# Seven instead of five edge groups gathered from x itself, and SyncE's wait for stored tables moved to slot 5

## Time and profile before

| | |
|---|---|
| median of 3 runs | 1107.77 us (1105.65 to 1108.65) |
| profiled execution | 1106.27 us |
| its span | 1104.5 us |
| POOL, gathers (L1068) | 741 from 3.7 us on, the last at 945.8 us |
| TensorE busy | 989.4 us, 90% of the span |
| VectorE, ScalarE, POOL busy | 824.7, 667.3, 739.1 us |

### The profile page before, as it was taken

How to read it: one execution, slowest core, us unless ns; L and a number is a source line. 1 busy time by engine, 2 the same in 40 slices (tenths; PEclk the granted TensorE clock), 3 DMA queues, 4 the chain that set the end, 5 groups by cost and what they waited for, 6 DMA issues and landing times.

```text
span 1104.5 us, 25223 instructions
## 1 busy us (share of the span) xinstructions
PE 989.4 (90%) x7011; PEld 737.0 (67%) x7041; DVE 824.7 (75%) x2919; ACT 667.3 (60%) x1736; POOL 739.1 (67%) x794
## 2 busy tenths in 40 slices
PE   5768988989799999989999999997888889899997
PEld 4456766767577677766767766666656667656786
DVE  6577877878778877877878878886877878645465
ACT  3334777888878787878877877643333233312664
POOL 7667777777777777777777777777777777200332
PEclk9798899999989999999999999998999999999998
DMA  8553443344434443344353444433454454545221
GB/s 207 153 140 94 98 105 90 93 108 106 107 86 112 105 113 96 97 102 127 91 122 91 107 121 112 107 97 91 99 147 95 110 143 105 139 132 161 83 58 41
DMA packets 126663, 121.24 MB, mean 110 GB/s; under 512 B 24238, under 2 KB 111077, under 8 KB 126517
## 3 DMA queue, kind: packets, MB, share of 16 engines
q1 hardware_dynamic: 99704, 69.74, 23.6%
q0 software_dynamic: 23712, 48.61, 18.2%
q10 hardware_dynamic: 3101, 1.21, 0.4%
HBM read 105.60 MB, written 13.88 MB: 108 GB/s over the span
## 4 chain that ended last, share of the span: by engine, by line
POOL 42%; PE 31%; issue 16%; DMA 5%; DVE 3%; ACT 1%; SPq 1%; ACTq 1%; DVEq 0%
POOL area L1068 42%; PE bank L1913 7%; PE bank L1693 5%; PE bank L1760 4%; PE bank L1788 3%; PE bank L1682 3%; PE bank L1633 3%; PE bank L1672 2%; DMA area<-zs_d,area 2%; PE bank L1621 1%; DMA area<-zr_d 1%; DMA adj_w<-in_dst_dram 1%; SPq L478 1%; DVE area L1364 0%; DMA area<-parts_d 0%
## 5 line engine op out<-in xcount | busy, mean ns | idle before, releaser
L1068 POOL DMA_INDIRECT area<-zs_d,area x721 | 687.0, 953 | 226.8 <-issue 218.3
L1254 DVE TENSOR_TENSOR_SCAN area<-area,bank 128x512 f32<-128x512 bf16 x196 | 249.6, 1274 | 172.3 <-PE bank L1633 151.4
L870 ACT CAST adj_w<-bank 128x325 f32 x391 | 176.7, 452 | 321.2 <-PE bank L1693 256.3
L1238 DVE TENSOR_SCALAR area<-area 128x325 bf16<-128x325 f16 x782 | 251.4, 322 | 0.0
L1693 PE MATMUL bank<-area 128*128 128x104 f32 x1564 | 228.1, 289 | 0.2
L1237 DVE TENSOR_SCALAR area<-area 128x128 bf16<-128x128 f16 x782 | 208.6, 267 | 12.5 <-PE bank L1693 11.2
L1693 PEld LDWEIGHTS bank<-area 128*128 128x128 f32 x1564 | 199.1, 199 | 10.4 <-issue 1.5
L1633 PE MATMUL bank<-ident,area 128*128 128x128 f32 x726 | 123.3, 294 | 52.6 <-DMA area<-zs_d,area 52.3
L1682 PE MATMUL bank<-area 128*128 128x325 bf16 x782 | 153.6, 310 | 11.4 <-ACT area L871 6.5
L923 ACT ACTIVATE area<-adj_w,node_c 128x512 bf16<-128x512 f32 x225 | 155.1, 744 | 0.0
L1633 PEld LDWEIGHTS bank<-ident,area 128*128 128x128 f32 x726 | 78.6, 144 | 97.4 <-DMA area<-zs_d,area 67.3
(11 more groups left out here) (174 smaller groups left out, 1029.8 us busy)
## 6 DMA issues: line engine op xcount, KB each, us to landing
area<-mask_d SPq DMA_DIRECT2D x195, 128.0 KB
area<-zs_d,area POOLq DMA_INDIRECT x721
area<-zs_d SPq DMA_DIRECT2D x640, 0.5 KB
area<-parts_d SPq DMA_DIRECT2D x20, 384.0 KB, 7.8
area<-wp_d SPq DMA_DIRECT2D x195, 9.0 KB
zr_d<-area SPq DMA_DIRECT2D x24, 128.0 KB
area<-zr_d SPq DMA_DIRECT2D x6, 512.0 KB, 4.7
area<-scale_d SPq DMA_DIRECT2D x10, 256.0 KB, 4.8
```

The source lines that it names most:

```text
L870: nc.scalar.copy(adj[:, :, bass.ds(at, W)], A_BANK[s % 2][:, 0:COLS].rearrange("p (h w) -> p h w", w=W))
L1068: pool.indirect_dma_start(gring[:, g % GR * 4 + s % 2 * 2 + u, :], None, x if g < RAW else zs_d[0:N, :], bass.IndirectOffsetOnAxis(ap=firs ...
L1238: nc.vector.tensor_scalar(hot_d[:, r, u, :], i_key[:, 0:COLS], key_n[:, u, s:s + 1], None, ALU.is_equal)
L1254: nc.vector.tensor_tensor_scan(S[:, g % 2, 0:n], mask[:, g % MR, 0:n], (G_BANK if g in PICKED else T_BANK[g % 2])[:, 0:n], S[:, (g + 1) % ...
```

## The change

`RAW` is 7. Groups 5 and 6 are gathered from x ahead of POOL's wait for `zs_st` and its branch; their raw buffers are two unused stretches of `aggT`. `raw_T` and `copy_raw` of group 4 move from slot 3 to slot 2, where those of group 5 join them, and those of group 6 stand in slot 3; on both engines they are now the first work of the slot (on TensorE, `raw_T(4)` stood behind the half pieces before, of which there are none so early). POOL's rule for the ring follows `RAW`: groups 9 and 10 wait for `raw_ps`, `t_ps` counts from group 11 on. SyncE's waits for `wp_st` and `zs_st` move from ahead of its loop into slot 5, behind `load_edges(5)`.

```diff
-RAW = 5
+RAW = 7
+RAW_SLOTS = ((4, 2), (5, 2), (6, 3))
...
         def raw(g):
-            return aggT[:, 512 * g:512 * g + 512] if g < 3 else raw_l[:, g - 3, :]
+            a = 512 * (g if g < 3 else g - 2)
+            return raw_l[:, g - 3, :] if g in (3, 4) else aggT[:, a:a + 512]
@@ SyncE @@
-                sp.wait_ge(wp_st, 48 * (BB - 1))
-                sp.wait_ge(zs_st, 16 * NX)
                 for k in range(NG + 5):
                     if 2 <= k < NG:
                         load_edges(k)
+                    if k == 5:
+                        sp.wait_ge(wp_st, 48 * (BB - 1))
+                        sp.wait_ge(zs_st, 16 * NX)
@@ ScalarE @@
                 for k in range(SLOTS):
-                    if k == 3:
-                        copy_raw(4)
+                    for g, at in RAW_SLOTS:
+                        if at == k:
+                            copy_raw(g)
                     if slots(k, 2) is not None:
                         adjacent(k - 2)
@@ TensorE @@
                 for k in range(SLOTS):
+                    for g, at in RAW_SLOTS:
+                        if at == k:
+                            raw_T(g)
...
-                    if k == 3:
-                        raw_T(4)
                     if 2 <= k < NG:
                         rows_T(k)
```

## The result

The changed kernel took 1109.1 us (median of 22 runs, 1107.18 to 1112.88) against 1107.64 us (22 runs) for the kernel before. The ratio is 1.0018, 95% interval 1.0009 to 1.0026: 1.0 to 2.9 us slower, inside the 0.3% that was called no change and inside the forecast range.

The account below looks back on a forecast made before the run. POOL's gathers bound the kernel; of 7.0 us of gaps 5.0 can go, but late rows_T waits leave D - 0.82 = +0.6 us: 1106.27 to 1106.9, or 1108.4 against the median. Range 1105.0 to 1111.0, 8 in 10.

Parts of the forecast that it names:

- No change that can be told, slightly slower, and why: Whole kernel: POOL's gain at groups 5 to 13 is lost waiting at 11 and 14; +0.6 us, chance 0.72.
- the part on what is late next: POOL at groups 11, 14, 15: waits for rows_T(7), rows_T(10), rows_T(11) take the gain back; worth D - 0.82 us.
- D: Delay from TensorE's slot 2, where raw_T(5) waits for copy_raw(4) ahead of rows_T(2); taken as 1.4 us, bounds -0.7 and 6.5.
- 67.2 + D: Start of group 11 on POOL, in us, after waiting for rows_T(7), instead of 70.28.
- SyncE's moved waits: nothing: SyncE behind its branch: the stretch there, not the stores, sets the mask of group 2; 0 us taken, up to 1.6 possible.
- D = 1.4: TensorE's delay from slot 2, carried through scan(4) and SyncE to rows_T(10) and rows_T(11); 1.4 us, between 0.95 and 1.9.
- the lower case: TensorE's slot 2: full clock returns at the same time, half of 1.9 us is won back, slot 3 is 0.95 us late.
- The branch stays between the raw gathers and the others: POOL: 2.3 us of flag load and branch move from group 5 to group 7, which starts at 45.2 us.
- +0.6: Group 15 on POOL: net delay in us with D = 1.4, carried unchanged to the end of the kernel.
- The rival in which all is won: POOL's three waits at groups 5, 8, 9 go and nothing binds afterwards; -5.0 us, 1102.8 us, chance 0.07.
- The slow rival (D = 6.5): TensorE stays at half clock through slot 3 because of pauses ahead of slot 2; +5.7 us, 1113.5 us, chance 0.07.

Follow-up runs that it names:

- the kernel with the late reload: Changed kernel with SyncE's table reload moved from slot 9 to 12 and its splitting to slots 14 to 17; 1.0000 against the kernel before.
- the hold alone taken away: Changed kernel with raw_T and copy_raw of groups 4, 5, 6 in slots 2, 3, 5, no raw_T behind a copy_raw ahead of rows_T(2); 0.9998 and 1.0014 against before.
- two holds: Changed kernel with raw_T and copy_raw of groups 4, 5, 6 all in slot 2, two raw_T behind copies ahead of rows_T(2); 1.0035 against before.

## Why the prediction was right

- *No change that can be told, slightly slower, and why.* Right in sign, in place, and in the wait that takes the gain back. The gaps of 3.35, 1.60 and 2.97 us went, and gaps at 11 and 14 came, named `rows_T`, as the part on what is late next had it. Group 14 started 0.28 us after `rows_T(10)` ended (85.56 and 85.84). Two steps came out otherwise. `rows_T(7)`, the wait ahead of group 11, ended at 67.37, 0.43 us later than before and not D later; POOL started 0.69 us behind it, at 68.06, where 0.26 was taken. The two errors go opposite ways, so the forecast of 67.2 + D, 68.6 us, was near by luck. And group 15 was not held by `rows_T(11)`, which ended at 89.90, only 0.49 us later than before; POOL was still busy with the four gathers of group 14 (beside the earlier trace rows):

```profile
89.24 0.66 PE L1637 MATMUL bank<-ident,area 128*128 128x128 f32 x4
```

The measurement told more than the 3.3 us that the forecast allowed it: its interval is 1.9 us wide and leaves out 1.
- *SyncE's moved waits: nothing.* Right, and shown by the kernel with that edit alone: the mask of group 2 at 42.10 us and not at 40.5, and the time within 0.13%.
- *D = 1.4.* It was not carried as one number. On the profile it is 1.6 at the start of slot 2, 0.65 at slot 3, 0.42 at slot 7, then 0.70 at SyncE's mask of group 6, 0.97 at the weights of group 10 and 1.26 at slot 10. More than half of the hold's price was won back in slot 2, as the lower case had it: the granted clock rose from half to full near 50.6 us, against 51.0 before. The stretch of the earlier trace rows in the changed kernel, with a mean clock of 0.55:

```profile
47.60:51.00 3.40, 3.40 (x10) 1.32 (x9) 0.66 (x1) 0.59 (x1) 2.64 (x3) 0.55 0.22 58
```

What was won back there came again behind it: the reload's issue took 3.54 us against 3.19, which the forecast carried over unchanged, and from the issue of the weights of group 10 to slot 10 it was 3.59 us against 3.30. That the 1.26 came near 1.4 is in part luck. At group 14 the sum is 1.25 (`rows_T(10)`) - 1.17 + 0.28 = +0.36, and group 15 has the same +0.36.
- *The branch stays between the raw gathers and the others.* Wrong. Group 7 started at 43.54 without a gap, not at 45.2. The flag load and the branch of POOL in the changed kernel, beside the earlier trace rows:

```profile
L415 POOLq TENSOR_LOAD <-large x1: 771/771/771, 34.7 to 34.7; - x1
```
```profile
L416 POOLq COMPARE_BRANCH  x1: 45/45/45, 35.8 to 35.8; - x1
```

POOL's sequencer ran ahead: it went through the branch at 35.8, while six raw gathers were still to start (the last at 42.29). In the kernel before nothing was queued any more when the table's wait ended, so the 2.3 us lay bare. The Trainium skill has the limit, in "Advanced Engine Details and Errata", section "Engine Queue Depths": 8 for GPSIMD. The trace agrees as far as it goes: at 33.2 us POOL's sequencer took the wait for the flag with the eight gathers of groups 5 and 6 still to start.

```profile
L414 POOLq EVENT_SEMAPHORE  x1: 17/17/17, 33.2 to 33.2; - x1
```

The error of 2.3 us changed nothing, since POOL waited longer than that ahead of group 11; where nothing binds later it would have counted.
- *The size.* +0.6 was forecast, +1.0 to +2.9 measured. At group 15 the profiles give +0.4 us for the changed kernel (mean 90.59 of three against 90.15 of two). The forecast carried group 15's delay to the end unchanged, and that step is not what happened. From group 15 to the end of the last gather 856.3 and 858.5 us passed in the two profiles of before, 858.4 to 859.2 in those of the changed kernel (857.4 to 861.1 in the others, five raw groups or seven), and from there to the end of the span 157.8 and 157.5 before, 155.7 to 157.2 after. In the first pair of profiles the last gather ended 3.3 us later and the span only 1.2. Some of the loss between can be named: VectorE's instructions of line 1317 meet POOL's gathers here as in the kernel with the late reload.

```profile
103.45 1.23 DVE L1317 TENSOR_TENSOR zs_r<-adj_w,zs_r 128x1024 fp32r<-128x1024 f32 x1 [1.95 <-ACT zs_r L915]
```
```profile
103.71 1.78 POOL L1072 DMA_INDIRECT area<-zs_d,area  x1 [0.30 <-issue]
```

The gathers that start under them cost 0.2 and 0.7 us more than 0.944 each in the two profiles of before, and 1.4, 1.4 and 1.1 in those of the changed kernel: it depends on when POOL comes by. No run was made for this alone. Another part lies outside the span, from the first to the last instruction, where no profile reaches: the time of an execution less its span is 1.8 to 2.1 us in all 125 on record with five raw groups, mean 1.85; with seven raw groups it is over 2.1 and up to 3.2 in 50 of 103, and its mean is 2.25 in the 22 of the changed kernel, 0.4 us more. What makes it is open, and so is the rest: the three profiled executions of the changed kernel lie 1.2 to 2.8 us under their medians. That the +0.6 came within 2.3 us of what was measured is in part luck.
- *Range and chances.* 1105.0 to 1111.0 held the 1109.1. The rival in which all is won did not occur in the changed kernel, nor with the hold alone taken away; even with the weights earlier and the reload in parts 4.1 us came of the 5.0. The slow rival (D = 6.5) did not occur; two holds cost 3.3 us more at group 15.

## What to carry to other kernels

A gap on the engine that bounds is worth only what its next wait leaves: list, for each later step, how long before its start its condition was met (here 1.17 and 1.08 us at groups 14 and 15 against a gain of 7), and follow that condition back to where the change puts its own new work. A producer that shares a buffer with its consumer's copy needs a slot in between, else the wait lands ahead of unrelated work (here two such waits cost 0.37% over none; the price of one isn't settled). Look for the first step of the chain, not for its loudest gap: five lines that issue one small load earlier gave 0.2%, which the removal of 7 us of gaps did not.

## What the runs showed of the hardware

- Behind its branch an engine was late by an amount of its own: POOL 1.1 us, SyncE 2.6, ScalarE 3.7 in the kernel before; 2.86 for ScalarE in the changed one. POOL's cost nothing in the changed kernel, where its sequencer reached it at 35.8 us with six gathers still to start.
- The gathers of one kernel take a different total from one profiled execution to the next: the time over 0.944 us each summed to 10.0 and 12.2 us in the two profiles of before and to 12.7, 14.4 and 11.7 in the three of the changed kernel. That is as large as the effect studied.
- In every profile here, a gather that started while VectorE's 128x1024 `TENSOR_TENSOR` that splits the table (line 1317 in the changed kernel, 1.2 us) ran and would have ended less than 0.8 us behind it ended 0.81 to 0.82 us behind it instead: up to 1.95 us for a gather of 0.944.
- The same small load of weights, issued at 42.5 us, landed at 46.05 in one profile and let TensorE start at 44.8 in another.
